# Stage one of a graph-mask kernel: two adjacency products turned together, normalised in place in a ring of four

## The chip, the cores and the metric

One Trainium2 chip, of which this kernel uses one core. The time is the device time of one launch in microseconds (us). TensorE is called PE, the loading of its stationary operand PEld, VectorE DVE, ScalarE ACT, GpSimd POOL and SyncE SP. SP only issues DMA transfers here.

## What is computed

The program is a small graph network. Its first stage makes the adjacency matrices. For 2048 samples, each of 1600 numbers, it multiplies by a masker of 1600 x 5000, adds a bias, takes the relu and divides every row of 50 by its sum:

```python
fusion = x.reshape(b, n * d)                       # 2048 x 1600
adj = einsum('bn,tnm->btm', fusion, masker_param) + masker_bias
adj = relu(adj).reshape(b, t, n, n)                # t = 2, n = 50
adj = adj / (adj.sum(axis=-1, keepdims=True) + 1e-06)
```

The second stage multiplies the adjacencies with the features and runs a gated unit on them (`r`, `z`, `ng`), and the third does batch norm, layer norm, a softmax over the nodes and a weighted sum. The change touches the first stage alone.

## The kernel before

**Tiles of stage one.** The samples are 16 tiles of 128. The 5000 columns are 10 groups of 500 (`GROUPS`, `GW`); a group is 10 rows of 50. A *product* is one sample tile by one column group: 128 x 500 in one bank of PSUM. There are 160, and they are numbered `c`. Two blocks of 8 tiles (`BLK`) are run: for each block and each group (`it`, 20 in all) the 8 tiles (`w`) are gone through while the group's part of the masker, `w_hi` and `w_lo`, stays in SBUF. Each fp32 operand is split in a high and a low part, so that a product takes three matmuls for each of 12 chunks of 128 rows and two for the last: 38 in all (line 443), in seven units of two chunks. `window` is PE's code for one product.

**After the product.** ACT takes the relu from PSUM to `u` (line 305). DVE sums the rows (line 355), adds the small constant, takes the reciprocal and multiplies `u` into `an` (line 363). PE turns `an` in four pieces of 128 x 125 into one bank of PSUM (`transposes`, line 425), ACT copies the bank to `at` (line 311), and SP stores that in HBM (`store_tile`, line 202), where stage two reads it. `u`, `an`, `at`, the product banks and the turn banks have two buffers each.

**The order on the engines** is written out by hand, and each engine goes through its list in order. PE turns product `c - 1` in the middle of window `c`, after unit 3 (`T_AT`), that is after 24 of its 38 matmuls. ACT's list for window `c` is: relu of `c - 1`, splits of x if there are any, in the last window of a group the splits of the next group's w (lines 285 and 286), and the copy of the turned `c - 1` among them. SP's list is loads of x and w, then the store of `c - 1`. In the first group (`it` 0) x is loaded tile by tile, one window ahead, through one raw buffer; in group 9 the 8 tiles of the second block come in the same way. A load of x waits in SP's list until the tile before it is split (`x_ready`).

**The waits around the turn.** PE waits for `an_ready` of product `c - 1` and for the copy of the turn before last (`at_ready`). ACT's relu waits for `an_ready` of the product that used its buffer before. DVE's multiply waits until the buffer of `an` was turned (`tr_done`). The copy waits until `at`'s buffer is stored (`at_stored`).

Of the kernel before, what the change touches and what calls it, by code (L numbers as in the profile page):

```python
# [25 lines left out]
P = 128  # L26
# [116 lines left out]
def stage1(nc, place, psum, ins, adjT, shared):  # L143
    xT, W, ident_d = ins["xT"], ins["W"], ins["ident"]
    with ExitStack() as ctx:  # L145
# [7 lines left out]
        w_hi = sb("w_hi", [P, KC, GW], fp32r)  # L153
        w_lo = sb("w_lo", [P, KC, GW], fp32r)
        ident = sb("ident_sb", [P, P])
        u = sb("u", [P, 2, GN, N])
        an = sb("an", [P, 2, GN, N])
        rows = sb("rows", [P, 3, GN])
        at = sb("at", [RK, 2, AK, P])
        assert free.at <= AT_WEIGHTS  # L160
# [7 lines left out]
        at_stored = shared.at_stored  # L168
        dve_step = sem("dve_step")
        g_product, zeroed, blocks_ready, wd_hi_ready = sem("g_product"), sem("zeroed"), sem("blocks_ready"), sem("wd_hi_ready")  # L170
        g_bank = psum[:, 4 * BANK:4 * BANK + 3 * D]

        def mm_out(c2):

            return psum[:, c2 * BANK:c2 * BANK + GW]

        def tr_out(c2):

            return psum[0:RK, (2 + c2) * BANK:(3 + c2) * BANK]

        block = ctx.enter_context(nc.Block())

# [1 line left out]
        def _(sp):  # L184
# [28 lines left out]
            for blk in range(BLOCKS):  # L213
                for it, group in p1_iters(sp, blk):
                    for w in range(BLK):
                        if isinstance(it, int) and it == 0 and w + 1 < BLK:
                            load_x(w + 1, 0)
                            load_x(w + 1, 1)
                        if not (isinstance(it, int) and it == ITERS - 1):
                            nxt = 0 if isinstance(it, int) and it % GROUPS == GROUPS - 1 else group + 1  # L220

                            for i in range(NU):
                                if w == (min(i + 1, BLK - 2) if isinstance(it, int) and it == 0 else 1):
                                    load_w(i, nxt, it * NU + i + 1)
                        c = it * BLK + w
                        if w > 0:
                            store_tile(c - 1, (w - 1) % 2, blk * BLK + w - 1, group)
                        elif not (isinstance(it, int) and it == 0):
                            if isinstance(it, int) and it % GROUPS == 0:
                                store_tile(c - 1, 1, blk * BLK - 1, GROUPS - 1)  # L230
                            else:
                                store_tile(c - 1, 1, blk * BLK + BLK - 1, group - 1)
# [15 lines left out]
            store_tile(ITERS * BLK - 1, 1, TILES - 1, GROUPS - 1)  # L248

        def split_x_hi(act, bt, half):  # L250
            act.wait_ge(x_loaded[half], 16 * (bt + 1))
# [46 lines left out]

        @block.scalar
        def _(act):  # L300
            def relu(c, c2, start=False):
                act.wait_ge(mm_done, c + 1)
                if not start:
                    act.wait_ge(an_ready, c - 1)
                nc.scalar.activation(u[:, c2].rearrange("p n m -> p (n m)"), mm_out(c2), ACT.Relu).then_inc(u_ready, 1)  # L305

            def evacuate(c, c2, start=False):
                act.wait_ge(tr_done, c + 1)
                if not start:
                    act.wait_ge(at_stored[c2], 8 * (c - c2))  # L310
                nc.scalar.copy(at[:, c2].rearrange("p k b -> p (k b)"), tr_out(c2)).then_inc(at_ready, 1)  # L311

            split_x_hi(act, 0, 0)
            for i in range(NU):
# [3 lines left out]
            for blk in range(BLOCKS):  # L318
                for it, group in p1_iters(act, blk):
                    static = isinstance(it, int)  # L320
                    for w in range(BLK):
                        c = it * BLK + w
                        split = w == BLK - 1 and not (static and it == ITERS - 1)
                        if not (static and it == 0 and w == 0):
                            relu(c - 1, (w - 1) % 2, start=static and it == 0 and w <= 2)
                        if static and it == GROUPS and w == 0:
                            for half in range(2):
                                split_x_hi(act, 2 * BLK - 1, half)
                        if static and it == 0 and w + 1 < BLK:
                            for half in range(2):  # L330
                                split_x_hi(act, w + 1, half)
                        if split:
                            for i in range(0, T_AT + 1):
                                split_w_hi(act, i, it + 1)
                        if not (static and it == 0 and w == 0):
                            evacuate(c - 1, (w - 1) % 2, start=static and it == 0 and w <= 2)
                        if split:
# [9 lines left out]
            relu(c, 1)  # L347
            evacuate(c, 1)

        @block.vector  # L350
        def _(dve):
            def normalise(c, c2, start=False):

                dve.wait_ge(u_ready, c + 1)
                nc.vector.tensor_reduce(rows[:, 0], u[:, c2], AX.X, ALU.add).then_inc(dve_step, 1)  # L355
                dve.wait_ge(dve_step, 3 * c + 1)
                nc.vector.tensor_scalar_add(rows[:, 1], rows[:, 0], EPS_ROW).then_inc(dve_step, 1)
                dve.wait_ge(dve_step, 3 * c + 2)
                nc.vector.reciprocal(rows[:, 2], rows[:, 1]).then_inc(dve_step, 1)
                dve.wait_ge(dve_step, 3 * c + 3)  # L360
                if not start:
                    dve.wait_ge(tr_done, c - 1)
                nc.vector.tensor_tensor(an[:, c2], u[:, c2], rows[:, 2].unsqueeze(2).to_broadcast([P, GN, N]),  # L363
                                        ALU.mult).then_inc(an_ready, 1)

            def weight_blocks(dve):
# [23 lines left out]
            for blk in range(BLOCKS):  # L390
                for it, group in p1_iters(dve, blk):
                    static = isinstance(it, int)
                    for w in range(BLK):
                        c = it * BLK + w
                        if not (static and it == 0 and w == 0):
                            normalise(c - 1, (w - 1) % 2, start=static and it == 0 and w <= 2)
# [18 lines left out]
            normalise(ITERS * BLK - 1, 1)  # L415

        @block.tensor
        def _(pe):
            def transposes(c, c2, start=False):
                pe.wait_ge(an_ready, c + 1)  # L420
                if not start:
                    pe.wait_ge(at_ready, c - 1)
                flat = an[:, c2].rearrange("p n m -> p (n m)")
                for k in range(AK):
                    last = nc.tensor.transpose(tr_out(c2)[:, k * P:(k + 1) * P], flat[:, k * RK:(k + 1) * RK], ident[:, :])  # L425
                last.then_inc(tr_done, 1)

            def window(it, w, blk, c, start=False, bank_free=False, none_before=False):
                pe.wait_ge(x_ready, 2 * (blk * BLK + w) + 1)
                if not bank_free:  # L430
                    pe.wait_ge(u_ready, c - 1)
                for i, (k0, k1) in enumerate(UNITS):
# [15 lines left out]
                        last.then_inc(w_used, 1)  # L448
                    if none_before and i == NU - 1:
                        pe.wait_ge(ident_loaded, 16)  # L450
                    if i == T_AT and not none_before:
                        transposes(c - 1, (w - 1) % 2, start=start)

            for blk in range(BLOCKS):
                if blk == 1:
# [2 lines left out]
                for it, group in pe_iters(pe, blk):  # L458
                    static = isinstance(it, int)
                    for w in range(BLK):  # L460
                        c = it * BLK + w
                        window(it, w, blk, c, start=static and it == 0 and w <= 2,
                               bank_free=static and it == 0 and w < 2, none_before=static and it == 0 and w == 0)
            transposes(ITERS * BLK - 1, 1)


def p1_iters(eng, blk):
# [1005 lines left out]
```

## Time and profile before

| | us |
|---|---|
| median of 3 runs | 2270.66 |
| lowest, highest run | 2262.55, 4165.84 |
| the profiled execution's own time | 2267.87 |
| its span (first to last instruction) | 2266.1 |
| stage one, by the last copy of a turned bank | ends at about 1460 |

One run of the three took nearly twice the time of the other two; the two others are 8 us apart. The page gives busy time by engine and cuts the span in 40 slices. The timeline gives every instruction's start and duration; matmuls are pipelined, so the time that one costs is the distance of its start from the next one's start, not its duration.

### The profile page before, as it was taken

The page shows a single profiled execution, that of the slowest core. Times are in us where ns is not written, and L with a number is a line of the kernel's source. Part 1 is how long each engine was busy: PE and PEld are TensorE (multiplying, and loading weights), DVE is VectorE, ACT ScalarE, POOL GpSimd, SP SyncE. Part 2 cuts the span into 40 slices and gives each one's busy share as a digit, 9 for nine tenths or more (in the row PEclk, how much of TensorE's full clock was granted, in tenths as well). Part 3 has the DMA queues.
Part 4 walks back from the last instruction along what each step waited for, and adds up shares of the span by engine and source line. Part 5 has one row for each costly group of instructions (what it writes and reads, how often), then busy time and mean ns, then how long its engine had stood idle before and what let it go on. Part 6 is the DMA issues. An engine that isn't in the chain of part 4 may idle for free. (4 is left out here: it accounts for less than half of the span.)

```text
span 2266.1 us, 34747 instructions
## 1 busy us (share of the span) xinstructions
PE 2196.3 (97%) x12302; PEld 1738.1 (77%) x12302; DVE 1086.5 (48%) x2177; ACT 961.4 (42%) x1639; POOL 135.4 (6%) x124
## 2 busy tenths in 40 slices
PE   8999999999999999999999999999999999986888
PEld 6888888888888888888888888777777777772333
DVE  4432233323335233322333133278888888884656
ACT  4322122212224122212222122278888888876551
POOL 0000000000000000000000000011101111004340
PEclk9999999999999999999999999999999999997899
DMA  6411222122224322122220223367676776746440
GB/s 215 154 54 64 94 91 90 29 93 90 90 91 144 107 91 93 43 77 91 95 89 28 93 93 72 103 166 197 187 198 180 194 193 183 200 150 194 119 119 5
DMA packets 341600, 264.00 MB, mean 116 GB/s; under 512 B 169318, under 2 KB 302854, under 8 KB 339846
## 3 DMA queue, kind: packets, MB, share of 16 engines
q1 hardware_dynamic: 323402, 225.63, 34.0%
q10 hardware_dynamic: 18144, 37.69, 5.1%
q8 instruction: 29, 0.48, 0.1%
q14 instruction: 25, 0.20, 0.0%
HBM read 195.59 MB, written 67.70 MB: 116 GB/s over the span
## 5 line engine op out<-in xcount | busy, mean ns | idle before, releaser
L443 PE MATMUL psum<-w_hi,x_lo 128*128 128x500 f32 x2080 | 821.2, 395 | 8.9 <-DVE w_lo L292 8.9
L443 PE MATMUL psum<-w_lo,x_hi 128*128 128x500 f32 (+1 forms) x2080 | 808.4, 389 | 0.0
L443 PE MATMUL psum<-w_hi,x_hi 128*128 128x500 f32 x1920 | 744.2, 388 | 0.0
L355 DVE TENSOR_REDUCE rows<-u 128x10 f32<-128x500 f32 x160 | 107.6, 673 | 889.6 <-ACT u L305 889.1
L443 PEld LDWEIGHTS psum<-w_hi,x_lo 128*128 128x128 f32 x2080 | 391.6, 188 | 83.7 <-issue 8.2
L443 PEld LDWEIGHTS psum<-w_lo,x_hi 128*128 128x128 f32 (+1 forms) x2080 | 391.9, 188 | 72.2
L443 PEld LDWEIGHTS psum<-w_hi,x_hi 128*128 128x128 f32 x1920 | 361.0, 188 | 73.0
L311 ACT COPY at<-psum 125x512 f32<-125x512 f32 x160 | 93.5, 585 | 676.4 <-PE psum L425 676.4
L305 ACT ACTIVATE u<-psum 128x500 f32<-128x500 f32 x160 | 93.8, 586 | 344.3 <-PE psum L443 344.3
L764 PE MATMUL psum<-adj_sb,xs_sb 100*64 100x100 f32 x2048 | 200.6, 350 | 1.6 <-PEq L145 1.6
L744 POOL TENSOR_TENSOR xg_lo<-xg_sb,xg_hi 128x400 fp32r<-128x400 f32 x64 | 67.0, 1050 | 1927.5 <-ACT xg_hi L593 1927.5
L764 PEld LDWEIGHTS psum<-adj_sb,xs_sb 100*64 100x64 f32 x2048 | 144.5, 149 | 45.6 <-issue 35.4
L627 ACT ACTIVATE r_gate<-psum,bias 64x400 f32<-64x400 f32 x256 | 151.0, 590 | 23.2 <-PE psum L791 21.0
L292 DVE TENSOR_TENSOR w_lo<-w_raw,w_hi 128x1000 fp32r<-128x1000 f32 x120 | 144.1, 1201 | 23.9 <-ACT w_hi L286 18.3
L286 ACT CAST w_hi<-w_raw 128x1000 fp32r<-128x1000 f32 (+1 forms) x140 | 135.9, 971 | 46.3 <-PE psum L443 44.6
L632 ACT ACTIVATE psum<-psum,bias 64x400 f32<-64x400 f32 x256 | 142.3, 556 | 13.2 <-DVE hG L687 6.8
L363 DVE TENSOR_TENSOR an<-u,rows 128x500 f32<-128x500 f32 x160 | 108.6, 679 | 6.9
L695 DVE BATCH_NORM_STATS2 stats<-hC 128x128 f32 (+1 forms) x400 | 88.4, 282 | 46.6 <-ACT hC L605 46.2
L425 PEld LDWEIGHTS psum<-ident_sb,an 128*125 128x125 f32 x640 | 94.6, 187 | 16.4 <-DVE an L363 3.0
L425 PE MATMUL psum<-ident_sb,an 128*125 128x128 f32 x640 | 96.1, 273 | 3.4 <-DVE an L363 3.4
L1101 DVE SCALAR_TENSOR_TENSOR pr<-h,nmu_sb,psum 128x512 f32<-128x512 f32 x100 | 70.5, 742 | 46.3 <-PE psum L1312 24.5
L672 DVE SCALAR_TENSOR_TENSOR n_in<-psum,bias,r_gate 128x400 f32<-128x400 f32 x128 | 79.6, 622 | 14.3 <-PE psum L797 13.6
(162 smaller groups left out, 2277.8 us busy)
## 6 DMA issues: line engine op xcount, KB each, us to landing
w_raw<-W SPq DMA_DIRECT2D x140, 500.0 KB, 7.9
adjT<-at SPq DMA_DIRECT2D x160, 250.0 KB
adj_sb<-adjT SPq DMA_DIRECT2D x32, 1250.0 KB
xs_sb<-xz SPq DMA_DIRECT2D x16, 1600.0 KB
hF<-hC ACTq DMA_DIRECT2D x96, 256.0 KB, 6.5
h<-hF SPq DMA_DIRECT2D x64, 256.0 KB, 4.2
xg_sb<-xg ACTq DMA_DIRECT2D x14, 800.0 KB, 8.0
h<-hF SPq DMA_DIRECT2D x48, 192.0 KB, 3.5
```

The lines of the kernel that those rows point to most:

```text
L286: nc.scalar.copy(w_hi[:, k0:k1, :], w_raw[:, k0:k1, :]).then_inc(w_hi_ready, 1)
L292: nc.vector.tensor_tensor(w_lo[:, k0:k1, :], w_raw[:, k0:k1, :], w_hi[:, k0:k1, :].bitcast(fp32), ALU.subtract).then_inc(w_ready, 1)
L305: nc.scalar.activation(u[:, c2].rearrange("p n m -> p (n m)"), mm_out(c2), ACT.Relu).then_inc(u_ready, 1)
L311: nc.scalar.copy(at[:, c2].rearrange("p k b -> p (k b)"), tr_out(c2)).then_inc(at_ready, 1)
L355: nc.vector.tensor_reduce(rows[:, 0], u[:, c2], AX.X, ALU.add).then_inc(dve_step, 1)
L363: nc.vector.tensor_tensor(an[:, c2], u[:, c2], rows[:, 2].unsqueeze(2).to_broadcast([P, GN, N]), ALU.mult).then_inc(an_ready, 1)
L425: last = nc.tensor.transpose(tr_out(c2)[:, k * P:(k + 1) * P], flat[:, k * RK:(k + 1) * RK], ident[:, :])
L443: last = nc.tensor.matmul(mm_out(w % 2), a[0:r, w, k, :], b[0:r, k, :], start=k == 0 and n == 0, stop=k == KF and n == 1)
L627: last = nc.scalar.activation(r_gate[half], rz_bank(pair)[half], ACT.Sigmoid, bias=bias[half, R_G:R_G + 1])
L632: last = nc.scalar.activation(z_bank[half], rz_bank(pair)[other], ACT.Sigmoid, bias=bias[other, Z_G:Z_G + 1])
L695: last = nc.vector.bn_stats(stats[:, bass.ds(tile, 1), c, :].rearrange("p i v -> p (i v)"), hC[:, c, :])
L764: last = nc.tensor.matmul(out_[SH * i:SH * i + SH, :, gi], xs[r][:, b, :], adj[r][:, :, b], start=True, stop=True)
```

## The change

- The turns of two products are done together: in every window with even `w`, after unit 3, eight turns (products `c - 2` and `c - 1`) stand in a row. Windows with odd `w` have none. At the end of the stage the last two products are turned together.
- `an` is gone. DVE multiplies in place, `u` to `u`, and `u` has four buffers in place of two. SBUF use is the same.
- There are four turn banks in PSUM (banks 2 to 5) in place of two; a small product that had bank 4 goes to bank 6.
- ACT's relu of `c` waits for the turn of product `c - 4` (`tr_done`), in place of `an_ready`. DVE's wait for `tr_done` is gone. PE waits for `an_ready` of both products at once, and for the copies of the pair two before.
- ACT copies two banks one behind the other in even windows; SP stores two tiles one behind the other in even windows and none in odd ones. `at` still has two buffers.

The core of the diff:

```diff
-        u = sb("u", [P, 2, GN, N])
-        an = sb("an", [P, 2, GN, N])
+        u = sb("u", [P, 4, GN, N])
...
-            def relu(c, c2, start=False):
+            def relu(c, c4):
                 act.wait_ge(mm_done, c + 1)
-                if not start:
-                    act.wait_ge(an_ready, c - 1)
-                nc.scalar.activation(u[:, c2].rearrange("p n m -> p (n m)"), mm_out(c2), ACT.Relu).then_inc(u_ready, 1)
+                wait(act, tr_done, c - 3)
+                nc.scalar.activation(u[:, c4].rearrange("p n m -> p (n m)"), mm_out(c4 % 2), ACT.Relu).then_inc(u_ready, 1)
...
-                        if not (static and it == 0 and w == 0):
-                            evacuate(c - 1, (w - 1) % 2, start=static and it == 0 and w <= 2)
+                        if w % 2 == 0 and not (static and it == 0 and w == 0):
+                            evacuate(c - 2, (w - 2) % 4)
+                            evacuate(c - 1, (w - 1) % 4)
...
-                if not start:
-                    dve.wait_ge(tr_done, c - 1)
-                nc.vector.tensor_tensor(an[:, c2], u[:, c2], rows[:, 2].unsqueeze(2).to_broadcast([P, GN, N]),
+                nc.vector.tensor_tensor(u[:, c4], u[:, c4], rows[:, 2].unsqueeze(2).to_broadcast([P, GN, N]),
...
-            def transposes(c, c2, start=False):
-                pe.wait_ge(an_ready, c + 1)
-                if not start:
-                    pe.wait_ge(at_ready, c - 1)
-                flat = an[:, c2].rearrange("p n m -> p (n m)")
-                for k in range(AK):
-                    last = nc.tensor.transpose(tr_out(c2)[:, k * P:(k + 1) * P], flat[:, k * RK:(k + 1) * RK], ident[:, :])
-                last.then_inc(tr_done, 1)
+            def transposes(c, w):
+                pe.wait_ge(an_ready, c)
+                wait(pe, at_ready, c - 4)
+                for c4 in ((w - 2) % 4, (w - 1) % 4):
+                    flat = u[:, c4].rearrange("p n m -> p (n m)")
+                    for k in range(AK):
+                        last = nc.tensor.transpose(tr_out(c4)[:, k * P:(k + 1) * P], flat[:, k * RK:(k + 1) * RK], ident[:, :])
+                    last.then_inc(tr_done, 1)
...
-                    if i == T_AT and not none_before:
-                        transposes(c - 1, (w - 1) % 2, start=start)
+                    if i == T_AT and w % 2 == 0 and not none_before:
+                        transposes(c, w)
```

PE's list in a window of the first group, around the turn, before. The rows are line, operation, output and inputs; `ident_sb` is the identity that a turn multiplies with.

```order
L443 MATMUL psum<-w_hi,x_hi 128x500
L425 MATMUL psum<-ident_sb,an 125x128 [waits at_ready,an_ready]
L425 MATMUL psum<-ident_sb,an 125x128 x3
L443 MATMUL psum<-w_hi,x_lo 128x500 [waits x_ready]
L443 MATMUL psum<-w_lo,x_hi 128x500
```

The same place in an even window now:

```order
L443 MATMUL psum<-w_hi,x_hi 128x500
L425 MATMUL psum<-ident_sb,u 125x128 [waits an_ready]
L425 MATMUL psum<-ident_sb,u 125x128 x7
L443 MATMUL psum<-w_hi,x_lo 128x500 [waits x_ready]
L443 MATMUL psum<-w_lo,x_hi 128x500
```

Eight turns stand where four stood, and the window before and behind it has 38 product matmuls and nothing else. There are as many turns as before.

ACT's list at the start of a looped group, two windows, before (L305 is the relu, L311 the copy of a turned bank; ALU rows count the loop's semaphore values):

```order
L304 REGISTER_ALU [waits mm_done]
L305 ACTIVATE u<-psum 128x500 [waits an_ready]
L310 REGISTER_ALU [waits tr_done]
L311 COPY at<-psum 125x512 [waits at_stored1]
L302 REGISTER_ALU
L304 REGISTER_ALU [waits mm_done]
L305 ACTIVATE u<-psum 128x500 [waits an_ready]
L310 REGISTER_ALU [waits tr_done]
L311 COPY at<-psum 125x512 [waits at_stored0]
```

And now:

```order
L83 REGISTER_ALU [waits mm_done]
L305 ACTIVATE u<-psum 128x500 [waits tr_done]
L309 REGISTER_ALU
L83 ISA [waits tr_done]
L311 COPY at<-psum 125x512 [waits at_stored0]
L311 COPY at<-psum 125x512 [waits at_stored1,tr_done]
L303 REGISTER_ALU
L83 REGISTER_ALU [waits mm_done]
L305 ACTIVATE u<-psum 128x500 [waits tr_done]
```

The two copies follow each other, behind the relu of the even window, and the odd window has the relu alone.

SP's list in the first group, before, from the load of the third x tile on (each x tile is two transfers):

```order
L190 DMA x_raw<-xT 128x1024 [waits x_ready]
L190 DMA x_raw<-xT 128x768 [waits x_ready]
L196 DMA w_raw<-W 128x1000 [waits w_ready]
L202 DMA adjT<-at 125x4x128 [waits at_ready]
L190 DMA x_raw<-xT 128x1024 [waits x_ready]
L190 DMA x_raw<-xT 128x768 [waits x_ready]
L196 DMA w_raw<-W 128x1000 [waits w_ready]
L202 DMA adjT<-at 125x4x128 [waits at_ready]
```

And now:

```order
L189 DMA x_raw<-xT 128x1024 [waits x_ready]
L189 DMA x_raw<-xT 128x768 [waits x_ready]
L195 DMA w_raw<-W 128x1000 [waits w_ready]
L189 DMA x_raw<-xT 128x1024 [waits x_ready]
L189 DMA x_raw<-xT 128x768 [waits x_ready]
L195 DMA w_raw<-W 128x1000 [waits w_ready]
L201 DMA adjT<-at 125x4x128 [waits at_ready] x2
L189 DMA x_raw<-xT 128x1024 [waits x_ready]
```

One x tile is no longer behind a store, and the next one is behind two.

## Rows read from the trace of the kernel before

**Rows 1.** The page: span, busy time of engines, and slices of 1/40 of the span.

```profile
span 2266.1 us, 34747 instructions
...
PE 2196.3 (97%) x12302; PEld 1738.1 (77%) x12302; DVE 1086.5 (48%) x2177; ACT 961.4 (42%) x1639; POOL 135.4 (6%) x124
...
PE   8999999999999999999999999999999999986888
```

**Rows 2.** Busy time by stretch: length, then PE, PEld, DVE, ACT, POOL; clock, DMA share, GB/s.

```profile
27.00:1447.00 1420.00, 1419.18 (x6609) 1191.30 (x6608) 451.77 (x829) 342.81 (x522) 0.00 (x0) 1.00 0.27 88
...
1460.00:1469.00 9.00, 6.42 (x47) 5.70 (x48) 1.06 (x2) 5.36 (x11) 4.04 (x4) 0.50 0.63 170
...
2070.50:2073.80 3.30, 3.30 (x17) 0.97 (x11) 0.00 (x0) 3.30 (x6) 2.87 (x4) 0.50 1.00 290
2075.00:2083.00 8.00, 5.31 (x20) 1.01 (x20) 0.00 (x0) 4.20 (x6) 6.43 (x6) 1.00 1.12 337
```

**Rows 3.** Waits from 27 to 1447 us, all engines: total, times, longest.

```profile
DVE rows L355 <- ACT u L305: 873.8, 132, 7.2
ACT at L311 <- PE psum L425: 668.4, 132, 5.3
...
PE psum L425 <- DVE an L363: 0.8, 1, 0.8
```

**Rows 4.** Timeline of PE around a turn: start, duration; a run's rows are merged.

```profile
702.32 0.39 PE L443 MATMUL psum<-w_hi,x_hi 128*128 128x500 f32 x1
702.55 0.60 PE L425 MATMUL psum<-ident_sb,an 128*125 128x128 f32 x4
702.90 0.47 PE L443 MATMUL psum<-w_hi,x_lo 128*128 128x500 f32 x1
703.21 0.39 PE L443 MATMUL psum<-w_lo,x_hi 128*128 128x500 f32 x1
...
711.33 0.39 PE L443 MATMUL psum<-w_hi,x_hi 128*128 128x500 f32 x1
```

**Rows 5.** Line 425 from 27 to 1447 us: instructions, busy us, mean ns.

```profile
L425 PE MATMUL psum<-ident_sb,an 128*125 128x128 f32 x628 | 94.2, 273 | 0.8 <-DVE an L363 0.8
```

**Rows 6.** Timeline, two turns that lie 70 windows apart.

```profile
89.42 0.60 PE L425 MATMUL psum<-ident_sb,an 128*125 128x128 f32 x4
...
720.58 0.60 PE L425 MATMUL psum<-ident_sb,an 128*125 128x128 f32 x4
```

**Rows 7.** Timeline of ACT and DVE behind a product, and its turn.

```profile
706.35 0.59 ACT L305 ACTIVATE u<-psum 128x500 f32<-128x500 f32 x1 [0.72 <-PE psum L443]
...
708.14 0.68 DVE L363 TENSOR_TENSOR an<-u,rows 128x500 f32<-128x500 f32 x1
...
711.56 0.60 PE L425 MATMUL psum<-ident_sb,an 128*125 128x128 f32 x4
```

**Rows 8.** Timeline where the second block begins (window 80).

```profile
738.97 0.39 PE L443 MATMUL psum<-w_hi,x_hi 128*128 128x500 f32 x1
740.18 0.70 PE L425 MATMUL psum<-ident_sb,an 128*125 128x128 f32 x4 [0.82 <-DVE an L363]
740.63 0.47 PE L443 MATMUL psum<-w_hi,x_lo 128*128 128x500 f32 x1
...
742.70 0.58 ACT L311 COPY at<-psum 125x512 f32<-125x512 f32 x1
...
744.09 0.59 ACT L305 ACTIVATE u<-psum 128x500 f32<-128x500 f32 x1 [0.81 <-PE psum L443]
```

**Rows 9.** Timeline in the first group: an x tile's load, its split, its use.

```profile
36.78 0.31 SPq L202 DMA_DIRECT2D adjT<-at  x1
37.13 1.11 SPq L190 DMA_DIRECT2D x_raw<-xT  x2
...
44.49 1.83 DVE L267 TENSOR_TENSOR x_lo<-x_raw,x_hi 128x1024 fp32r<-128x1024 f32 x2 [2.91 <-ACT x_hi L257]
...
47.94 0.39 PE L443 MATMUL psum<-w_hi,x_lo 128*128 128x500 f32 x1
```

**Rows 10.** DMA from 36.5 to 45.5 us: GB/s in 40 slices, packets.

```profile
GB/s 0 0 0 0 5 80 82 80 155 150 191 130 241 294 369 339 269 307 360 389 413 363 342 371 377 403 319 274 149 194 157 148 98 160 107 89 53 18 18 0
DMA packets 937, 1.69 MB, mean 187 GB/s; under 512 B 53, under 2 KB 553, under 8 KB 937
```

**Rows 11.** Timeline at the end of stage one.

```profile
1458.98 0.77 PE L425 MATMUL psum<-ident_sb,an 128*125 128x128 f32 x4 [2.56 <-DVE an L363]
...
1459.79 0.58 ACT L311 COPY at<-psum 125x512 f32<-125x512 f32 x1 [2.74 <-PE psum L425]
...
1461.35 0.93 PE L764 MATMUL psum<-adj_sb,xs_sb 100*64 100x100 f32 x8 [1.59 <-PEq L145]
```

**Rows 12.** Timeline of PE in the kernel's first microseconds.

```profile
9.19 0.62 PE L443 MATMUL psum<-w_hi,x_hi 128*128 128x500 f32 x1
9.61 0.62 PE L443 MATMUL psum<-w_hi,x_lo 128*128 128x500 f32 x1
```

More of the change, by code:

```diff
@@ L170, in stage1, with tr_out @@
         g_product, zeroed, blocks_ready, wd_hi_ready = sem("g_product"), sem("zeroed"), sem("blocks_ready"), sem("wd_hi_ready")
-        g_bank = psum[:, 4 * BANK:4 * BANK + 3 * D]
+        g_bank = psum[:, 6 * BANK:6 * BANK + 3 * D]
         def mm_out(c2):
             return psum[:, c2 * BANK:c2 * BANK + GW]
-        def tr_out(c2):
-            return psum[0:RK, (2 + c2) * BANK:(3 + c2) * BANK]
+        def tr_out(c4):
+            return psum[0:RK, (2 + c4) * BANK:(3 + c4) * BANK]
         block = ctx.enter_context(nc.Block())
@@ L225, in _ @@
                         c = it * BLK + w
[L226 to L232, printed above, removed]
+                        for back in (2, 1) if w % 2 == 0 else ():
+                            if w > 0:
+                                store_tile(c - back, back % 2, blk * BLK + w - back, group)
+                            elif not (isinstance(it, int) and it == 0):
+                                if isinstance(it, int) and it % GROUPS == 0:
+                                    store_tile(c - back, back % 2, blk * BLK - back, GROUPS - 1)
+                                else:
+                                    store_tile(c - back, back % 2, blk * BLK + BLK - back, group - 1)
                         if isinstance(it, int) and it == GROUPS - 1 and blk + 1 < BLOCKS:
@@ L247, in _ @@
                                 load_xg(sp, shared, ins, 0)
-            store_tile(ITERS * BLK - 1, 1, TILES - 1, GROUPS - 1)
+            for back in (2, 1):
+                store_tile(ITERS * BLK - back, back % 2, TILES - back, GROUPS - 1)
         def split_x_hi(act, bt, half):
@@ L300, in _, with evacuate @@
         def _(act):
-            def relu(c, c2, start=False):
+            def relu(c, c4):
                 act.wait_ge(mm_done, c + 1)
-                if not start:
-                    act.wait_ge(an_ready, c - 1)
-                nc.scalar.activation(u[:, c2].rearrange("p n m -> p (n m)"), mm_out(c2), ACT.Relu).then_inc(u_ready, 1)
-            def evacuate(c, c2, start=False):
+                wait(act, tr_done, c - 3)
+                nc.scalar.activation(u[:, c4].rearrange("p n m -> p (n m)"), mm_out(c4 % 2), ACT.Relu).then_inc(u_ready, 1)
+            def evacuate(c, c4):
+                c2 = c4 % 2
                 act.wait_ge(tr_done, c + 1)
-                if not start:
-                    act.wait_ge(at_stored[c2], 8 * (c - c2))
-                nc.scalar.copy(at[:, c2].rearrange("p k b -> p (k b)"), tr_out(c2)).then_inc(at_ready, 1)
+                wait(act, at_stored[c2], 8 * (c - c2))
+                nc.scalar.copy(at[:, c2].rearrange("p k b -> p (k b)"), tr_out(c4)).then_inc(at_ready, 1)
             split_x_hi(act, 0, 0)
@@ L324, in _ @@
                         if not (static and it == 0 and w == 0):
-                            relu(c - 1, (w - 1) % 2, start=static and it == 0 and w <= 2)
+                            relu(c - 1, (w - 1) % 4)
                         if static and it == GROUPS and w == 0:
@@ L346, in _, with normalise @@
             c = ITERS * BLK - 1
-            relu(c, 1)
-            evacuate(c, 1)
+            relu(c, 3)
+            evacuate(c - 1, 2)
+            evacuate(c, 3)
         @block.vector
         def _(dve):
-            def normalise(c, c2, start=False):
+            def normalise(c, c4):
                 dve.wait_ge(u_ready, c + 1)
-                nc.vector.tensor_reduce(rows[:, 0], u[:, c2], AX.X, ALU.add).then_inc(dve_step, 1)
+                nc.vector.tensor_reduce(rows[:, 0], u[:, c4], AX.X, ALU.add).then_inc(dve_step, 1)
                 dve.wait_ge(dve_step, 3 * c + 1)
@@ L395, in _ @@
                         if not (static and it == 0 and w == 0):
-                            normalise(c - 1, (w - 1) % 2, start=static and it == 0 and w <= 2)
+                            normalise(c - 1, (w - 1) % 4)
                         if static and it == GROUPS and w == 0:
@@ L414, in _, with window @@
                                                     ALU.subtract).then_inc(shared.wd_ready, 1)
-            normalise(ITERS * BLK - 1, 1)
+            normalise(ITERS * BLK - 1, 3)
         @block.tensor
         def _(pe):
-            def transposes(c, c2, start=False):
-                pe.wait_ge(an_ready, c + 1)
-                if not start:
-                    pe.wait_ge(at_ready, c - 1)
-                flat = an[:, c2].rearrange("p n m -> p (n m)")
-                for k in range(AK):
-                    last = nc.tensor.transpose(tr_out(c2)[:, k * P:(k + 1) * P], flat[:, k * RK:(k + 1) * RK], ident[:, :])
-                last.then_inc(tr_done, 1)
-            def window(it, w, blk, c, start=False, bank_free=False, none_before=False):
+            def transposes(c, w):
[6 more added lines that the diff above has]
+                    last.then_inc(tr_done, 1)
+            def window(it, w, blk, c, bank_free=False, none_before=False):
                 pe.wait_ge(x_ready, 2 * (blk * BLK + w) + 1)
@@ L461, in _ @@
                         c = it * BLK + w
-                        window(it, w, blk, c, start=static and it == 0 and w <= 2,
-                               bank_free=static and it == 0 and w < 2, none_before=static and it == 0 and w == 0)
-            transposes(ITERS * BLK - 1, 1)
+                        window(it, w, blk, c, bank_free=static and it == 0 and w < 2, none_before=static and it == 0 and w == 0)
+            transposes(ITERS * BLK, 0)
 def p1_iters(eng, blk):
```

## The prediction, written before the changed kernel ran

> **What bounds the kernel now.** I read the page of the profile first. PE is busy for 2196.3 of 2266.1 us, and its slices stand at 9 over nearly the whole span [rows 1]. So the question for stage one is only what PE spends there. The view by stretch confirms it: from 27 to 1447 us PE is busy for 1419.18 of 1420.00 us, at a granted clock of 1.00, while DVE is busy for 451.77 and ACT for 342.81 us [rows 2]. The table of waits shows who waits for whom: DVE waits 873.8 us for the relu, ACT 668.4 us for the turn, and PE waits for neither, but for one wait of 0.8 us in 1420 [rows 3]. Both helpers are idle for more than half the time. Work or waits taken from them buy nothing; only time on PE counts.
>
> The last view is PE's timeline around one turn, and it is the one to read closely. The durations mislead here: a turn lasts 273 ns and there are 628 of them in the stretch [rows 5], which looks like 94 us. But they overlap. Four of them in a row last 0.60 us together [rows 4], so their starts are (0.60 - 0.273) / 3 = 0.109 us apart. Between the turns the product matmuls are 0.2256 us apart: 36 of them from 703.21 to 711.33 [rows 4].
>
> **What the turns cost PE.** From the matmul at 702.32 to the one at 703.21 lie 0.89 us [rows 4]. Two product matmuls are 0.451 and four turns 0.436, together 0.887. So entering and leaving the turns costs 0.003 us, which is within the rounding of the rows. The first matmul behind the turns lasts 0.47 in place of 0.39 us, but it also starts early, 0.35 us behind the first turn where four steps of 0.109 would be 0.44; the two effects cancel in the start of the one after. A second way to the same number, from the long run: two turns that are 70 windows apart are 631.16 us apart [rows 6], 9.0166 us each. 38 matmuls by 0.2256 and 4 turns by 0.109 are 9.009. What is left is 0.008 us, and it takes in all that a window has beside its matmuls. The switch between the kinds of work therefore costs 0.003 to 0.008 us.
>
> **The change, part by part.**
>
> *Eight turns in every second window.* The number of turns stays at 640. 80 of the 160 places where PE goes over to turns and back are gone, at 0.003 to 0.008 us each: 0.2 to 0.6 us less. I take 0.4 less, the middle, since the two views are equally near. The cost of a turn inside a run is 0.109 us in the middle of four, and I take the same for the middle of eight. It cannot fall much below that; even if the second four cost nothing, which no row suggests, it would be 80 by 0.436 = 35 us.
>
> *The place of the wait.* PE now waits, in even windows, for the product that has just ended, as before: the turn of c - 1 stands after unit 3 in both. In a common window the relu of it starts at 706.35, the multiply ends at 708.14 + 0.68 = 708.82, and the turn starts at 711.56 [rows 7]: 2.7 us to spare. The product c - 2 was ready a window earlier. Odd windows lose the wait. So the cost is nothing, covered by the 24 matmuls that stand ahead of the turn. The one place without cover is window 80, where PE goes from the matmul at 738.97 to the turn at 740.18: 1.21 us in place of 0.23, because ACT and DVE first split a late x tile [rows 8]. That window is even, its lists on ACT and DVE have the same work ahead of the multiply, and it keeps its 1.0 us.
>
> *In place multiply, ring of four.* The multiply has the same size and moves the same bytes; DVE has over half its time free. The relu of c waits for the turn of c - 4, which was done three or four windows earlier: satisfied. The banks are four, so PE's wait for a copy is for a pair that was turned four windows earlier: satisfied.
>
> *Two copies in a row on ACT.* The relu that is queued behind the second copy frees a product bank for PE, and PE needs that bank a whole window after the product's end; the second copy is 0.58 us [rows 11] and a window 9.0. In window 80 the copy is late: it starts at 742.70 and the next relu at 744.09 [rows 8]. With a second copy of 0.58 the relu still comes at 744.1. So the cost is nothing. The cover is ACT's idle time; without it, a pair would cost 0.58 us.
>
> *Two stores in a row, and the loads behind them on SP.* In the first group an x tile is loaded in the window before its use. Those of windows 4 and 6 now have two stores ahead of them. For window 4 the first half of the tile is issued at 37.13, directly behind the store at 36.78; its split into x_lo starts at 44.49, the first half being two thirds (1024 of 1536 columns) of the 1.83 us, so it is done at 45.7, and PE uses it at 47.94 [rows 9]: 2.2 us to spare. The second copy (0.58) and the second store's issue (0.31) delay the load by 0.9 us. The tile of the second store is 125 x 512 numbers of 4 bytes, 250 KB, more in the queues: at the mean 187 GB/s of that stretch 1.3 us, at the 241 to 413 GB/s of its middle slices [rows 10] about 0.8 us. That is 1.7 to 2.2 us against 2.2. So the cost is 0, and I keep 0.5 us a tile, 1.0 in all, as the upper bound. The other tiles have no store ahead of them and may come earlier, which buys nothing, since PE was not waiting for them [rows 3].
>
> *The end of the stage.* The last window loses four turns (0.44 less), and behind the wait for the last multiply stand eight (0.44 more). ACT's first copy can run when the first four are turned, at 1459.79 as now [rows 11]; the second copy adds 0.58 us ahead of stage two. Sum: 0.58 - 0.44 = 0.14 more. SP has one more store to issue ahead of stage two's loads, 0.3 us; stage two starts on data loaded earlier.
>
> **The sum**, against the profiled execution's 2267.87 us: - 0.4 (fewer changes of work) + 0 (waits, copies, x loads) + 0.1 (end) = 2267.6 us. The profiled execution lies between the two ordinary runs, 2262.55 and 2270.66 (the latter is the median only because of the third at 4165.84), so I keep 2267.6. Differences below about 2%, 45 us, can't be told from no change on this kernel's runs.
>
> **The rivals.**
>
> *The clock falls at the long turns (slower).* Eight turns are 0.87 us in which PE does no product matmul. If the clock fell to its half level after each, the price would be this: the shortest half-level stretch that I looked up holds at 0.50 from 2070.5 to 2073.8, and is over by 2075 [rows 2], so at least 3.3 us. At the half level product matmuls would be some 0.42 us apart, as they are in the first microseconds [rows 12], against 0.2256: each microsecond loses 0.46, a stretch 1.5 us, 80 stretches 122 us, and the time would be 2390 us. It decides (45 us) once 30 of the 80 places are hit. Against it: with four turns in every window the granted clock was 1.00 over 1420 us [rows 2], and this includes window 80, where idle time and four turns together keep PE from product matmuls from 739.20, where the next one would have started, to 740.63 [rows 8], 1.4 us, longer than eight turns would. At the stage's end the clock was at 0.50 from 1460 on, but after 2.56 us of idle time. The Trainium skill (TensorE: Matmul & The Clock Gate, Part 4: PE-mode transpose) says that the full rate does not engage for transpose-mode work, as it does not count as busy in the same way. By that rule the change goes in the dangerous direction, and the time would be that of this rival in place of the sum; the trace has turns only four at a time, and does not show a fall behind them. Chance 3%.
>
> *The turns cost more than their starts show (faster).* If the page's durations were the true cost, or if the second four hid behind the first, up to 35 us would go: 2233 us, which is 1.5% and so still not over 2%. For it stands only the 0.47 us of the matmul behind the turns; against it both sums above, which close to 0.008 us. Chance 3%. Beyond 2% would need more than the second four turns' whole time: 1%.
>
> *The x tiles or the pair of stores come late (slightly slower).* The mechanism is the full queue in even windows. If the delay of the two x tiles is twice the 2.2 us worked out above, each comes 2.2 us too late: 4.4 us, 2272 us. The store's landing is in no row; if `at` were the bound, ACT would wait, but PE has two pairs of banks before it does. Chance 10%, within 2%.
>
> *The change does nothing measurable*: this is the forecast itself. Chance 83%.
>
> **How the numbers follow.** The likeliest case is 2267.6, with the spread of ordinary runs, 4 us to each side, a clock stretch at the stage's end that may begin a step earlier or later (3.3 us by 0.46, 1.5 us), and the x tiles' 1 to 4.4 us upward. That gives 2260 to 2276. The other cases outside it hold 7%. Faster by over 2%: 1%. Slower by over 2%: 3%. Within 2%: 96%.
>
> **What would show it.** PE's eight turns should last 0.273 + 7 x 0.109 = 1.04 us as one run. Odd windows should be 8.57 us and even ones 9.45, together 18.03. If the pair of windows is clearly shorter than 18.03, the switch cost was read wrongly. The row of slices and the stretch from 27 to 1447 us should show the clock at 1.00; any 0.5 there is the slower rival. PE should wait for DVE once in that stretch, at window 80. A wait of PE for x_lo (line 267) between 40 and 70 us would be the third rival. ACT's second copy at the end of the stage should put stage two's start at about 1461.3 again. What would make the prediction wrong is a turn in a run of eight at another price than in a run of four, a thing this trace can't show.

## The result, and the profile after

The changed kernel takes 2314.21 us (median of 5 runs, 2310.18 to 2314.48), the kernel before 2267.43 (median of 5, one of which took 4165.84 and is left out of the ratio). The ratio is 1.0203, with a 95% interval of 1.0188 to 1.0218. It is slower, clear of noise, where no change was forecast; whether by more than 2% is not settled, since 1.02 lies inside the interval. The profiled execution has a span of 2312.7 us, 46.6 more than [rows 1].

The page of the changed kernel, the rows that answer to [rows 1], and two queues of its third part:

```profile
span 2312.7 us, 34431 instructions
...
PE 2209.5 (96%) x12302; PEld 1745.3 (75%) x12302; DVE 1089.8 (47%) x2177; ACT 957.3 (41%) x1639; POOL 135.4 (6%) x124
...
PE   8999999999999999999999999899988988986888
...
q8 instruction: 29, 0.48, 0.1%
q14 instruction: 50, 0.41, 0.1%
```

The first 25 slices, which are stage one, look as before. The new 8s stand from the 26th on, in stage two, whose code in the source the change did not touch. And the queue q14, which fetches instructions, has 50 packets; on the page of the kernel before its row reads `q14 instruction: 25, 0.20, 0.0%`. The view by stretch says the same of stage one (columns as in [rows 2]):

```profile
27.00:1447.00 1420.00, 1419.18 (x6596) 1189.16 (x6595) 450.81 (x827) 338.38 (x520) 0.00 (x0) 1.00 0.26 88
```

PE is busy for the same 1419.18 us at the full clock, but it gets 13 fewer instructions done in them: 6596 against 6609. That is the smaller of two losses. The larger shows in the table of waits:

```profile
DVE m_lo L661 <- issue: 35.3, 5, 7.2
...
PE psum L790 <- DVE m_lo L661: 35.5, 6, 7.0
```

Five times in stage two, DVE stands still for about 7.1 us (7.2 at most) in front of line 661 though the profile shows nothing that it waits for ("issue"), and PE waits for DVE. The kernel before has no such row. DVE's timeline at one of the five places:

```profile
1615.17 1.01 DVE L705 STREAM_TRANSPOSE hT<-hG 128x800 f32<-128x800 f32 x1
1623.36 0.57 DVE L661 TENSOR_TENSOR m_lo<-psum,m_hi 128x400 fp32r<-128x400 f32 x1 [7.18 <-issue]
```

The same two instructions in the kernel before, where line numbers are one higher:

```profile
1613.32 1.01 DVE L706 STREAM_TRANSPOSE hT<-hG 128x800 f32<-128x800 f32 x1
1614.25 0.54 DVE L662 TENSOR_TENSOR m_lo<-psum,m_hi 128x400 fp32r<-128x400 f32 x1
```

Between the two lies the branch that closes DVE's loop of stage two. The rows of the loop's own line, before and then after, give the length of an iteration: its branch runs six times, and goes back five times.

```profile
L727 DVEq COMPARE_BRANCH  x6: 50/56/63, 1613.4 to 1964.5; - x6
```

```profile
L726 DVEq COMPARE_BRANCH  x6: 55/62/72, 1615.6 to 2010.1; - x6
```

Five iterations take 351.1 us before and 394.5 after: 43.4 of the 46.6 us. Each is 8.7 us longer, and DVE's stillness is 7.1 of that (35.3 in five). PE stands still too while DVE does, and its clock falls to the half level, as the stretch that holds the end of the first stall shows against the iteration ahead of it. The other 1.6 us fit that half clock; no run separates them.

```profile
1540.00:1618.00 78.00, 77.02 (x653) 60.96 (x651) 66.61 (x147) 68.00 (x129) 9.41 (x9) 1.00 0.79 200
1619.00:1629.00 10.00, 5.01 (x22) 4.40 (x22) 4.21 (x7) 3.55 (x7) 0.00 (x0) 0.51 0.75 178
```

The DMA view gives q14's packets. In one iteration of the changed kernel, from 1618 to 1697 us:

```profile
q14 instruction: 5, 0.04, 0.2%
```

In the same iteration of the kernel before, 1613 to 1683 us, q14 has no row at all. So code is fetched anew in every iteration, five packets of 8192 bytes, where before none was. The 25 packets more on the page are five for each of the five branches back. Narrower windows of the same view place them: from 1615 to 1623.3 us, in the stall, come two, one more by 1627, and two between there and 1695.

### The profile page after: what moved, and what is told of

It reads as the page before. It is cut to its first block and busy times, and to the rows that moved or that the text cites. A ratio compares the mean times of both kernels' runs of the same rounds, so it can differ in the third digit from the quotient of the medians.

```text
span 2312.7 us, 34431 instructions
## 1 busy us (share of the span) xinstructions
PE 2209.5 (96%) x12302; PEld 1745.3 (75%) x12302; DVE 1089.8 (47%) x2177; ACT 957.3 (41%) x1639; POOL 135.4 (6%) x124
## 5 line engine op out<-in xcount | busy, mean ns | idle before, releaser
L305 ACT ACTIVATE u<-psum 128x500 f32<-128x500 f32 x160 | 94.0, 588 | 638.0 <-PE psum L443 638.0
L311 ACT COPY at<-psum 125x512 f32<-125x512 f32 x160 | 86.0, 590 | 378.3 <-PE psum L425 378.3
L363 DVE TENSOR_TENSOR u<-u,rows 128x500 f32<-128x500 f32 x160 | 108.6, 679 | 5.4
L790 PE MATMUL psum<-m_hi,wd_lo 64*128 64x400 f32 x256 | 59.4, 461 | 40.0 <-DVE m_lo L661 35.5
L661 DVE TENSOR_TENSOR m_lo<-psum,m_hi 128x400 fp32r<-128x400 f32 x128 | 70.7, 553 | 41.9 <-issue 35.3
```

The lines of the kernel that those rows point to most:

```text
L305: nc.scalar.activation(u[:, c4].rearrange("p n m -> p (n m)"), mm_out(c4 % 2), ACT.Relu).then_inc(u_ready, 1)
L363: nc.vector.tensor_tensor(u[:, c4], u[:, c4], rows[:, 2].unsqueeze(2).to_broadcast([P, GN, N]), ALU.mult).then_inc(an_ready, 1)
```

## Where the instructions lie

Why should code of stage two be fetched anew when only stage one changed? The diff takes out DVE's wait for `tr_done` and the arithmetic for it. In the compiled lists the stage-two loop of DVE begins at instruction 596 before and at 550 after, and its body has 289 instructions in both. The traces bear this out: DVE runs 289 instructions from one branch to the next, and with every loop body counted once, 46 fewer stand ahead of the loop in the changed kernel. By the 16 KiB or 256 instructions of the page of the Trainium skill that is named below, an instruction has 64 bytes, and a packet of 8192 bytes would hold 128; this is an estimate. By place within such a block the loop's head moved from 84 to 38 (596 and 550, modulo 128; the start of the list has an unknown offset in memory, so these are places relative to each other).

The theory to test: a body of 289 spans three blocks or four, by where it begins. With three, all of it would stay in DVE's instruction memory; with four, and the block behind fetched ahead, something would be thrown out and the head would have to be fetched at each branch back. Of 128 places 32 would be bad. The rival: the changed stage one disturbs stage two in another way, by its stores, its PSUM banks or the clock.

The Trainium skill (Runtime: NRT & Kernel Launch, Instruction fetch mechanics) describes such a stall: a taken branch whose target is not among the pages held must wait for a fetch. The trace agrees: the stall stands at the branch back, about 7.1 us each time, and two packets of instructions come in it.

## Experiments on the fetch

The tool for them is an instruction that does nothing: DVE raises an unused semaphore, n times, in the idle time of one window of stage one.

```diff
+                        if static and it == GROUPS and w == 4:
+                            for _ in range(46):
+                                dve.sem_inc(filler, 1)
```

**Changed kernel, 46 idle instructions** (the loop back at its old place):

> The changed kernel with 46 DVE instructions that only raise an unused semaphore, put in the idle time of one window of stage one; they set DVE's code of stage two back to the place that it has in the kernel before (loop head at instruction 596 of DVE's list, in place of 550). Fetch theory: DVE's idle time of about 7 us at each of five loop ends of stage two goes, and the instruction queue 14 falls from 33 fetches in stage two to about 9; time 2270 us, which is the kernel before plus what stage one's windows cost (3.7 us by the trace). Rival, that stage one's new stores, banks or turns disturb stage two: nothing changes, 2314 us.

Measured: 2269.73 us, 1.0013 of the kernel before (1.0004 to 1.0022). The stalls are gone: line 665, which is that of `m_lo` in this file, waits only 6.6 us for ACT, once, and q14 has 10 packets from 1465 to 2050 us.

```profile
L665 DVE TENSOR_TENSOR m_lo<-psum,m_hi 128x400 fp32r<-128x400 f32 x128 | 70.5, 551 | 6.6 <-ACT m_hi L600 6.6
```

```profile
q14 instruction: 10, 0.08, 0.0%
```

So 46 instructions that do nothing win back 44 of the 47 us that the change cost.

**Changed kernel, 128 idle instructions** (one block further, same place within it):

> The changed kernel with 128 such instructions, a whole fetch block of 8192 bytes, if blocks are of 128 instructions of 64 bytes. Fetch theory with blocks of 128: the loop lies as badly as in the changed kernel, 2312 to 2318 us. If the number of instructions or their total mattered in another way, or the block were larger, the time would be near 2270 us. Rival (stage one disturbs stage two): 2314 us too; it is told apart by the other runs.

Measured: 2311.62 us, 1.0194 (1.0179 to 1.0210), with 33 packets of q14 in the same stretch and 35.3 us of "issue". More idle instructions, and no gain: what counts is the place within 128.

**Kernel before, 82 idle instructions** (the bad place, without the change):

> The kernel before with 82 such instructions: 82 - 128 = -46, so its loop lies in the fetch blocks as the changed kernel's does (head at 678, 550 plus one block). Fetch theory: five stalls of about 8.7 us on DVE in stage two, 2308 to 2314 us, with nothing of the change in it. Rival: 2267 us.

Measured: 2308.97 us, 1.0183 (1.0168 to 1.0199). Its timeline has the stall, 7.20 us where the changed kernel has 7.18:

```profile
1611.49 1.01 DVE L710 STREAM_TRANSPOSE hT<-hG 128x800 f32<-128x800 f32 x1
1619.69 0.57 DVE L666 TENSOR_TENSOR m_lo<-psum,m_hi 128x400 fp32r<-128x400 f32 x1 [7.20 <-issue]
```

The rival falls here: nothing of the change is in this kernel.

**Kernel before, 46 idle instructions**, the control:

> Control: the kernel before with 46 such instructions, loop head at 642. If the bad places are a range of about 32 of 128, as the 289 instructions of the body against four blocks of 128 would have it, this one is good: 2267 us. If merely adding instructions costs, it would stand above it.

Measured: 2265.43 us, 0.9994 (0.9985 to 1.0003). The idle instructions themselves cost nothing.

**The width of the bad range**, changed kernel with 16 and with 112 idle instructions, one run each:

> The changed kernel with 16 idle DVE instructions ahead of stage two. By the fetch theory a body of 289 instructions touches four blocks of 128 instead of three when its head lies in the last 32 slots of a block. In slots counted from the compiled list (the start of the list itself has an unknown offset) the places known so far are: 38 bad (changed), 84 good (before), 2 good (before with 46). This one is at 54. With a bad range 32 wide that holds 38, exactly one of this run and the next is bad: one near 2312 us with about 33 fetches in stage two, one near 2270 us.

> The changed kernel with 112 idle DVE instructions, which is 16 slots less in the next block: place 22. Exactly one of this and the run at place 54 is bad, by the fetch theory. If both are bad the bad range is wider than 32, and four blocks held at once don't explain it.

Measured: 2314.36 and 2269.68 us, with 33 and 10 packets. Exactly one is bad. Together:

| kernel | loop head (modulo 128) | q14 packets, 1465 to 2050 us | us |
|---|---|---|---|
| before + 46 | 642 (2) | 10 | 2265.4 |
| changed + 112 | 662 (22) | 10 | 2269.7 |
| changed | 550 (38) | 33 | 2314.2 |
| changed + 128 | 678 (38) | 33 | 2311.6 |
| before + 82 | 678 (38) | 33 | 2309.0 |
| changed + 16 | 566 (54) | 33 | 2314.4 |
| before | 596 (84) | 11 | 2267.4 |
| changed + 46 | 596 (84) | 10 | 2269.7 |

The bad range begins between 22 and 38 and ends between 54 and 84, which 32 fits. Blocks of 256 do not fit: a body of 289 would span one more of them from 32 places in a row, but modulo 256 the bad heads are 38, 54 and 166, and 84, 130 and 150 between them are good. The same page of the Trainium skill gives blocks of 16 KiB or 256 instructions; for DVE the runs show packets of 8192 bytes and heads that fit 128, and the runs decide. What the runs show is that the head's place decides; what is held and what is thrown out is the theory's, and no run tells which blocks the five packets are.

**The loop pinned to a block's start**, with no idle instructions:

```diff
-            with dve.Fori(1, TILES // 2 - 1) as it:
+            with nc.Fori(1, TILES // 2 - 1, engines=(mybir.EngineType.DVE,), head_slot={mybir.EngineType.DVE: 0}) as its:
+                it = its
```

> The changed kernel with DVE's loop of stage two pinned to the start of a fetch block, with no idle instructions. Fetch theory: no stalls at the loop's ends, 2270 us as the run with 46 idle instructions. If the alignment to the block were not what counts, 2314 us.

Measured: 2275.52 us, 1.0041 (1.0027 to 1.0055). The five stalls are gone, but I had expected 2270: entering the loop now costs one. The trace has one more branch on DVE there, at 1548.3 us; that it jumps over padding ahead of the pinned head is my reading.

```profile
1548.25 1.01 DVE L705 STREAM_TRANSPOSE hT<-hG 128x800 f32<-128x800 f32 x1
1555.19 0.57 DVE L661 TENSOR_TENSOR m_lo<-psum,m_hi 128x400 fp32r<-128x400 f32 x1 [5.93 <-issue]
```

**The loop at its bad place, with a prefetch hint** for the branch back (the same line, with `hint_back_edge=True` in place of the slot; it adds one instruction at the head of each iteration, so the body has 290):

> The changed kernel, its loop left at the bad place, with a prefetch hint for the branch back at the head of each iteration on DVE. If the stall is the late fetch of the loop's first block, the hint should take most of the 7 us at each of five loop ends: 2275 to 2290 us. If the stall is all four blocks coming one behind another, the hint takes only the first of them and the time stays above 2295 us.

Measured: 2269.11 us, 1.0018 (1.0007 to 1.0029), better than I expected, and q14 at 10 packets. The branch back then costs DVE nothing that shows:

```profile
1616.17 1.01 DVE L705 STREAM_TRANSPOSE hT<-hG 128x800 f32<-128x800 f32 x1 [0.34 <-DVE hG L686]
1617.10 0.54 DVE L661 TENSOR_TENSOR m_lo<-psum,m_hi 128x400 fp32r<-128x400 f32 x1
```

I had thought of the hint as an earlier fetch. It does more: the fetches do not happen. How it keeps the blocks is open.

## Experiments on the turns

What stage one itself costs is the 3.1 us between the changed kernel with 46 idle instructions (2269.73) and the kernel before (2266.67 on the same chip). PE's timeline of the changed kernel around two runs of eight, and the last matmul (97 rows) of each window:

```profile
701.69 1.04 PE L425 MATMUL psum<-ident_sb,u 128*125 128x128 f32 x8
...
705.51 0.39 PE L443 MATMUL psum<-w_lo,x_hi 97*128 97x500 f32 x1
714.14 0.39 PE L443 MATMUL psum<-w_lo,x_hi 97*128 97x500 f32 x1
...
719.77 1.03 PE L425 MATMUL psum<-ident_sb,u 128*125 128x128 f32 x8
```

A pair of windows is 719.77 - 701.69 = 18.08 us, where it was 2 x 9.0166 = 18.033. The run of eight lasts 1.04 us, as forecast. The odd window, with 38 product matmuls and nothing else, is 705.51 to 714.14 = 8.63 us: 0.227 a matmul, not 0.2256. The even window is the rest, 9.45 us, as forecast. So product matmuls behind a run of eight are slower, not the turns. 79 pairs by 0.047 are 3.7 us. Four kernels test where it comes from; all have the 46 idle instructions, so that the stalls of stage two are out of it.

**Eight turns in two fours**, twelve product matmuls between them (`transposes` now takes the products that it turns, and waits for the later of them):

```diff
-                    if i == T_AT and w % 2 == 0 and not none_before:
-                        transposes(c, w)
+                    if i in (T_AT - 2, T_AT) and w % 2 == 0 and not none_before:
+                        transposes(c, w, (2,) if i < T_AT else (1,))
```

> The changed kernel with 46 idle DVE instructions (so stage two is as before), and the eight turns of an even window in two runs of four: product c - 2 after unit 1, product c - 1 after unit 3. If what stage one still costs (3.1 us by the run with 46 idle instructions, 47 ns per pair of windows by its trace) comes from eight turns in one row, the pair falls to about 18.03 us and the time to 2266.7. If it comes from odd windows without turns, it stays at 18.08 us and 2269.7.

Measured: 2266.08 us, 1.0000 (0.9991 to 1.0009). The pair is down and the odd window is 8.58:

```profile
700.55 0.60 PE L429 MATMUL psum<-ident_sb,u 128*125 128x128 f32 x4
703.93 0.39 PE L447 MATMUL psum<-w_lo,x_hi 97*128 97x500 f32 x1
712.51 0.39 PE L447 MATMUL psum<-w_lo,x_hi 97*128 97x500 f32 x1
...
718.57 0.60 PE L429 MATMUL psum<-ident_sb,u 128*125 128x128 f32 x4
```

Its odd windows have no turns either, so it is not that.

**Each product turned alone**, with the in-place multiply and the rings of four kept (copies and stores are one a window again as well):

```diff
-                for c4 in ((w - 2) % 4, (w - 1) % 4):
+                for c4 in ((w - 1) % 4,):
...
-                    if i == T_AT and w % 2 == 0 and not none_before:
+                    if i == T_AT and not none_before:
```

> The changed kernel with 46 idle DVE instructions, its in-place multiply, ring of four and four turn banks kept, but each product turned, copied and stored alone in its window, as before. If the pairing is what costs in stage one, the pair of windows is 18.03 us and the time 2266.7. If the in-place multiply or the banks cost, it stays at 2269.7.

Measured: 2267.02 us, 1.0005 (0.9996 to 1.0014). The times tell no cost of the ring and the in-place multiply. The trace does show one:

```profile
87.40 0.60 PE L427 MATMUL psum<-ident_sb,u 128*125 128x128 f32 x4
...
701.10 0.60 PE L427 MATMUL psum<-ident_sb,u 128*125 128x128 f32 x4
```

Between the two lie 68 windows, 9.025 us each, where it was 9.0166: a pair is 18.05 us and not the 18.03 expected, 1.3 us over the stage. So the pairing in one row is most of the 3 us but not shown to be all of it. Nor do the parts simply add up, since the two fours have the same ring and stand at 18.03.

**The run of eight later**, after unit 5, and **the two fours nearer**, after units 2 and 3 (one run each):

> The changed kernel with 46 idle DVE instructions and the run of eight turns after unit 5 instead of unit 3, so 2 product matmuls stand behind it in its window in place of 14. Theory that a run of eight slows a fixed stretch of product matmuls behind it: the pair of windows stays at 18.08 us, and the excess over the split kernel's windows (8.573 and 9.456) stands wholly in the odd window behind. Rival, that it hangs on how the run lies to the windows' borders: the pair changes.

> As the run with the turns in two fours, but with six product matmuls between the two fours (after units 2 and 3) in place of twelve. If eight turns without a break are what costs, the pair is 18.03 us as with twelve. If eight turns within a short time cost, it is nearer 18.08.

Measured: 2271.37 and 2267.74 us, against one run of the kernel before at 2263.63. The first has a second loss: in the first group PE waits for `x_lo` at 48.05 and at 69.15 us, 4.4 us in all, in windows 4 and 6, whose x loads stand behind two stores that now come later. The later run gives a pair of 18.06 us and an odd window of 8.61, the nearer fours one of 18.04:

```profile
710.93 1.03 PE L429 MATMUL psum<-ident_sb,u 128*125 128x128 f32 x8
712.03 0.39 PE L447 MATMUL psum<-w_lo,x_hi 97*128 97x500 f32 x1
720.64 0.39 PE L447 MATMUL psum<-w_lo,x_hi 97*128 97x500 f32 x1
...
728.99 0.27 PE L429 MATMUL psum<-ident_sb,u 128*125 128x128 f32 x1
```

```profile
699.39 0.60 PE L429 MATMUL psum<-ident_sb,u 128*125 128x128 f32 x4
...
717.43 0.60 PE L429 MATMUL psum<-ident_sb,u 128*125 128x128 f32 x4
```

Neither theory comes out clean. If a run of eight slowed a fixed stretch behind it, moving it would have left 18.08; if only an unbroken eight mattered, the near fours would have given 18.03, and from 87.60 to 701.19 us their 34 pairs are 18.05 each. What can be said: the mean spacing of product matmuls in a window differs by up to 0.6% with where the turns stand, the unbroken eight after unit 3 is the worst of the placements tried, and fours twelve matmuls apart are as good as the kernel before. Why is open.

## Why the prediction was wrong, point by point

**The step that failed** stands in no term of the sum. The working costed what each edit does in stage one, and took stage two over unchanged; the order of instructions on DVE was looked at only for waits. The edit "DVE's wait for `tr_done` is gone" was costed at nothing because DVE is idle half the time ("work or waits taken from them buy nothing"). As work, that is right. As code it removes 46 instructions ahead of a loop of 289, and this moved the loop to a place where every branch back stalls: 43.4 us. Slower by over 2% had only the clock as its mechanism, with 3%. The clock did fall, but in stage two, at the stalls, and it does not where they are taken out; the runs of eight turns never lowered it (1.00 from 27 to 1447 us).

**The term that had the wrong sign** is "fewer changes of work, 0.4 less". The two views agreed that a switch costs 0.003 to 0.008 us, and from that the gain followed. It assumed that product matmuls keep their 0.2256 us whatever stands ahead of them. They do not: 3.7 us more by the trace, 3.1 by the runs. (The pair that was forecast is 8.57 + 9.45 = 18.02 us, not the 18.03 written; the difference changes nothing.) The text named an eight at another price as what would make it wrong; it was the matmuls behind the eight that changed.

**What held.** What bounds stage one, and that the helpers' time is worth nothing there. The price of a turn: eight in 1.04 us. The waits: PE waits for DVE once in the stretch, 0.8 us, at the start of the second block, as before. The x tiles of the first group come in time in spite of two stores ahead of them; PE has no wait for x. But the mechanism of the rival with the late x tiles is real: in the run with the turns two units later, PE waits for the very two tiles that it named. The end of the stage: the forecast was 0.14 us more. From the start of the last turns to stage two's first matmul it is 2.99 us against 2.37 [rows 11], less the 0.44 us that the last window is shorter: 0.18 more. That it comes so close is in part luck, as the same stretch takes 2.37 to 2.81 us in three traces of the kernel before, with and without idle instructions:

```profile
1459.98 1.14 PE L425 MATMUL psum<-ident_sb,u 128*125 128x128 f32 x8 [2.56 <-DVE u L363]
1462.97 2.97 PE L763 MATMUL psum<-adj_sb,xs_sb 100*64 100x100 f32 x32 [1.86 <-PEq L145]
```

**The sum as it should have been**: 43.4 us (five branches back by 8.7) and 3.7 us (79 pairs by 0.047) are 47.1; the spans differ by 46.6. Read along the two traces, the difference is -2.6 us up to the end of the second product, +3.6 over the other 158 windows, +0.6 at the stage's end, +0.6 from there to the loop's first branch, +43.4, and +1.0 behind the last branch. The -2.6 is mostly chance: the second product's last matmul starts from 28.5 to 29.7 us in three traces of the kernel before, and from 27.1 to 30.0 in seven of the changed one.

No version beats the kernel before. The best with the change in it, the two fours with 46 idle instructions, equals it.

## What to carry to other kernels

Before a change is costed at nothing, count the instructions it adds or removes on each engine ahead of a loop that it does not touch, and see whether the loop's body spans one more fetch block than before. "issue" in front of the first instruction of a loop body, together with a rising count of instruction packets, is the sign of it, and a prefetch hint at the branch back cures it here as well as 46 idle instructions do (2269.1 and 2269.7 us against 2314.2), without a count that the next edit upsets. To judge an edit in a kernel with large loops, compare it with the loop held at the same place; here the change itself is worth 3 us of loss, and the placement 44.

## What the runs showed that I had not expected

- A loop of 289 DVE instructions costs nothing or 8.7 us per iteration, by its head's place, and the heads tried fit a period of 128 instructions. 7.1 us is DVE's stillness; the rest fits the half clock of PE behind it.
- The hint removes the fetches (10 packets against 33), it does not merely start them sooner.
- Pinning the loop costs one stall of 5.93 us on entry.
- The spacing of product matmuls on a PE that never waits moved between 0.2256 and 0.227 us with the place of the turns among them, and with the ring of four alone a pair of windows went from 18.03 to 18.05 us.
